# Mask products and shared banks for the score maxima, a re-measured planner, and another order of the query blocks

## The reference, cut to what matters

```
scores = q @ k^T                      # per head, 2048 x 2048
scores = where(j <= i, scores, -inf)  # causal
scores += slope[h] * (j - i)          # attention a only
w = softmax(scores / 4);  out = (w @ v) @ Wo + bo
x = x + out
```

## Time and profile before

| | us |
|---|---|
| median of 3 runs (2376.23 to 2398.64) | 2376.96 |
| the profiled execution | 2381.28 |
| its span, first to last instruction | 2379.6 |
| attention cores up to the last turn | 87 to 543 and 1282 to 1731 |
| from there to the experts' first work | 543 to 591 and 1731 to 1779 |
| the experts and the projections | the rest |
| mean granted clock of PE | 0.912 |

### The profile page before, as it was taken

How to read it: one execution, slowest core, us unless ns; L and a number is a source line. 1 busy time by engine, 2 the same in 40 slices (tenths; PEclk the granted TensorE clock), 3 DMA queues, 4 the chain that set the end, 5 groups by cost and what they waited for, 6 DMA issues and landing times. The chain is left out here.

```text
span 2379.6 us, 33652 instructions
## 1 busy us (share of the span) xinstructions
PE 2189.3 (92%) x11000; PEld 1442.5 (61%) x11000; DVE 1619.7 (68%) x3265; ACT 962.1 (40%) x1333; POOL 727.2 (31%) x722
## 2 busy tenths in 40 slices
PE   5699999997799998999987999999977999999998
PEld 4444444444588887888764444444445888878886
DVE  6578887874665556666566788878746666666665
ACT  1145756475222232322341467564742322322222
POOL 4000101002355554555340001010023555545553
PEclk9678988898899999999996689888988999999999
DMA  3640404000133332333126404040002333333332
GB/s 136 130 58 2 55 2 55 2 2 18 65 122 108 108 104 91 108 110 115 66 97 125 55 2 54 2 54 2 2 8 77 120 108 108 104 122 110 108 108 77
DMA packets 59956, 172.46 MB, mean 72 GB/s; under 512 B 7912, under 2 KB 13560, under 8 KB 57360
## 3 DMA queue, kind: packets, MB, share of 16 engines
q1 hardware_dynamic: 59852, 171.14, 27.5%
HBM read 150.35 MB, written 20.23 MB: 72 GB/s over the span
## 5 line engine op out<-in xcount | busy, mean ns | idle before, releaser
L850 ACT ACTIVATE probs_t<-exp_banks 128x1024 f32<-128x1024 f32 (+3 forms) x640 | 539.3, 895 | 346.0 <-PE exp_banks L1099 340.6
L976 PE MATMUL exp_banks<-xT_t,e_hi_t 128*128 128x512 f32 x2080 | 656.0, 396 | 15.2 <-DVE inter_t L1227 13.4
L1363 DVE TENSOR_REDUCE chunk_max_t<-max_bank 128x1 f32<-128x512 f32 x768 | 488.5, 683 | 95.8 <-PE max_bank L1078 93.1
L976 PEld LDWEIGHTS exp_banks<-xT_t,e_hi_t 128*128 128x128 f32 x2080 | 393.2, 190 | 107.8 <-issue 13.1
L659 POOL TENSOR_TENSOR e_hi_t<-e_raw_t,ones_t 128x512 fp32r<-128x512 f32 (+1 forms) x260 | 283.9, 1092 | 534.3 <-PE pv_bank L976 455.2
L976 PE MATMUL exp_banks<-xT_t,e_lo_t 128*128 128x512 f32 x1040 | 412.0, 396 | 0.0
L1236 DVE TENSOR_TENSOR i_lo_t<-inter_t,i_hi_t 128x512 fp32r<-128x512 f32 (+1 forms) x264 | 249.6, 945 | 184.4 <-ACT i_hi_t L787 184.4
L787 ACT ACTIVATE i_hi_t<-inter_t 128x512 fp32r<-128x512 f32 (+1 forms) x264 | 166.9, 632 | 508.4 <-DVE inter_t L1231 508.4
L753 POOL TENSOR_SCALAR_AFFINE_SELECT probs_t<-probs_t 128x512 f32<-128x512 f32 x128 | 81.4, 638 | 909.3 <-ACT probs_t L850 909.3
L1113 PE MATMUL pv_bank<-probs_t,values_t 128*32 128x512 f32 (+3 forms) x2560 | 327.1, 587 | 14.2 <-POOL probs_t L753 10.1
L1227 DVE TENSOR_TENSOR inter_t<-exp_banks,silu_t 128x512 f32<-128x512 f32 (+1 forms) x264 | 182.3, 690 | 201.5 <-ACT silu_t L783 198.8
(11 more groups left out here) (200 smaller groups left out, 2061.7 us busy)
## 6 DMA issues: line engine op xcount, KB each, us to landing
wide_t<-route_rows SPq DMA_DIRECT2D x128, 512.0 KB, 4.4
e_raw_t<-in_experts SPq DMA_DIRECT2D x130, 384.0 KB, 4.3
Qp_t<-q_parts SPq DMA_DIRECT2D x36, 256.0 KB
Kp_t<-k_parts SPq DMA_DIRECT2D x24, 256.0 KB
q_parts<-part_hi_t SPq DMA_DIRECT2D x16, 256.0 KB, 2.6
q_parts<-part_lo_t SPq DMA_DIRECT2D x16, 256.0 KB, 3.1
k_parts<-part_hi_t SPq DMA_DIRECT2D x16, 256.0 KB, 3.0
k_parts<-part_lo_t SPq DMA_DIRECT2D x16, 256.0 KB, 3.4
```

Source lines behind the costliest of these rows:

```text
L850: act.activation(probs[:, e % NP, 2 * p:2 * p + 2, off:QB], exp_banks[p][:, :, off:QB], ACT.Exp, scale=D ** -0.5).then_inc(exp_done, 1)
L976: last = pe.matmul(out, stationary(a, k), moving(c, k), start=start and n == 0, stop=stop and n == len(order) - 1, skip_group_check=not (s ...
L1363: dve.tensor_reduce(to, bank[:, 0:n], AX.X, ALU.max).then_inc(max_free, 1)
```

## The change

1. **Mask products.** The custom instruction goes. The mask is now added by PE: after the product of a diagonal piece, two more products (a half of an identity, bf16, by a half of the triangle `cut`, 128 and 64 columns wide) accumulate -1e30 onto the last 128 keys. DVE uses the plain reduction throughout. POOL makes the bf16 copies at the start, eight more small copies, and PE waits for them before the first core.
2. **Shared banks.** The 16 diagonal pieces of a block share 10 banks: the two 256-wide pieces of a head half in one bank (one reduction for both), a 384-wide and a 128-wide piece in one bank (two reductions), each 512-wide one alone.
3. **The plan's model** has other durations, models the two halves of PE and POOL's cut, and lets `turned` come 2600 ns after the turn. `LOAD` stays 12000 ns.
4. **The order of blocks** becomes 0123, 3210, 3210, 3201 for groups 0 to 3. The load of group g + 1 still follows the turn of the third block in order.

```diff
-UP, DOWN = list(range(NB)), list(range(NB))[::-1]
-BLOCKS = [(g, b) for g in range(G) for b in (UP if g < G - 1 else DOWN)]
+UP, DOWN, LAST = [0, 1, 2, 3], [3, 2, 1, 0], [3, 2, 0, 1]
+ORDER = [UP, DOWN, DOWN, LAST]
+BLOCKS = [(g, b) for g in range(G) for b in ORDER[g]]
...
+def bank_items(b):
+
+    full = [(hh, [(p, r, c)]) for r in range(TPB) for c in range(b) for p in range(2) for hh in range(2)]
+    diagonal = [(hh, [(0, 1, b), (1, 1, b)]) for hh in range(2)]
+    diagonal += [(hh, [(p, 2, b), (p, 0, b)]) for p in range(2) for hh in range(2)]
+    diagonal += [(hh, [(p, 3, b)]) for p in range(2) for hh in range(2)]
+    return full + diagonal
...
-    SIGNAL, ROWS_BACK, LOAD = 250, 7000, 12000
+    SIGNAL, ROWS_BACK, LOAD, CYCLE = 45, 2600, 12000, 2.3
+    WEIGHTS, TURN, CTX, PROJECT = 183, 300, 550, 1600
...
+        items = [("max", g, b, k) for k in range(len(bank_items(b)))]
+        if number:
+            items.insert(2, ("turn", *BLOCKS[number - 1]))
...
+            _, g, b, number = item
+            hh, parts = bank_items(b)[number]
+            issue = halves(start, [(hh, part_width(b, r, c)) for _, r, c in parts])
+            for _, _, c in parts:
+                ended[hh] += 60 * (c == b)
+            pe = max(ended)
+            dve = max(dve, ended[hh] + SIGNAL)
+            if parts[0][1:] == (1, b):
+                dve += 152 + QB / 0.96
+            else:
+                for _, r, c in parts:
+                    dve += 152 + part_width(b, r, c) / 0.96
...
             turned[item[1:]] = dve + ROWS_BACK
+            if item[2] == ORDER[g][NB - 2] and 1 <= g < G - 1:
+                loaded[g + 1] = max(turned[item[1:]], scored_group.get(g - 1, dve)) + LOAD
...
         elif kind == "qk":
-            act = max(act, pe + SIGNAL, free) + 2 * n / 1.2 + 60
+            act = max(act, pe + SIGNAL, free) + 170 + 2 * n * 0.832
...
-                    if b == NB - 2 and 1 <= g < G - 1:
+                    if b == ORDER[g][NB - 2] and 1 <= g < G - 1:
...
+                            if c == b:
+                                rows = slice(hh * HALF, (hh + 1) * HALF)
+                                for a in range(2):
+                                    last = pe.matmul(bank[:, end - P + a * HALF:end], ident16[rows, a, :],
+                                                     cut16[rows, a, a * HALF:P], start=False, stop=a == 1)
...
-                            dve.tensor_tensor_reduce(masked[k % 2][:, 0:n], bank[:, 0:n], diag_mask[:, QB - n:QB],
-                                                     1.0, VLOW, ALU.add, ALU.max, to).then_inc(max_free, 1)
+                                op = dve.tensor_reduce(chunk_max[:, slot, 2 * p + hh, r, c:c + 1], bank[:, begin:end],
+                                                       AX.X, ALU.max)
```

More of the change, by code:

```diff
@@ L73, with part_width @@
 LOADS_AFTER = {"K0": "fresh", "Q1": 0, "K1": 1}
+def bank_items(b):
[4 more added lines that the diff above has]
+    return full + diagonal
+def part_width(b, r, c):
+    return P * (r + 1) if c == b else QB
 def core_plan():
-    SIGNAL, ROWS_BACK, LOAD = 250, 7000, 12000
+    SIGNAL, ROWS_BACK, LOAD, CYCLE = 45, 2600, 12000, 2.3
+    WEIGHTS, TURN, CTX, PROJECT = 183, 300, 550, 1600
     maxima = []
     for number, (g, b) in enumerate(BLOCKS):
[L92 to L98, removed]
+        items = [("max", g, b, k) for k in range(len(bank_items(b)))]
+        if number:
+            items.insert(2, ("turn", *BLOCKS[number - 1]))
+        maxima += items
     maxima.append(("turn", *BLOCKS[-1]))
@@ L141, in ready, with halves, whole @@
             return None
-        return exps.get((item[4], 1))
+        if (item[4], 1) not in exps:
+            return None
+        return max(exps[item[4], 1], pv_bank_free) if item[3] == 0 else exps[item[4], 1]
+    def halves(start, widths):
+        at_issue = start
+        for hh, n in widths:
+            weights = max(at_issue, began[hh])
+            began[hh] = max(weights + WEIGHTS, ended[hh] + 8)
+            ended[hh] = began[hh] + n / CYCLE
+            at_issue = weights + 3
+        return at_issue
+    def whole(end):
+        began[:], ended[:] = [end, end], [end, end]
+        return end
     while any(at[k] < len(s) for k, s in enumerate(streams)):
@@ L149, in core_plan @@
                 if when is not None:
-                    when = max(when, pe)
+                    same = mode == "halves" and s[at[k]][0] in ("max", "qk")
+                    when = max(when, issue if same else max(issue, pe))
                     if best is None or when < best[0]:
@@ L195, in core_plan @@
             n = width(b, j)
-            pe = start + n / 2.4 + 20
+            issue = halves(start, [(0, n), (1, n)])
+            pe = max(ended)
             free = products[e - NP] if e >= NP else 0
-            act = max(act, pe + SIGNAL, free) + 2 * n / 1.2 + 60
[L199 to L202, removed]
+            act = max(act, pe + SIGNAL, free) + 170 + 2 * n * 0.832
+            exp_bank_free[scored % 2] = act + 50
+            scored += 1
+            exps[e, p] = act + 50
+            if p == 1 and j >= TPB * b:
+                pool = max(pool, act + 50) + 740
+                exps[e, p] = pool + 50
+            if p == 1 and b == ORDER[g][-1] and j == TPB * (b + 1) - 1:
+                scored_group[g] = pe
         elif kind == "pv":
@@ L397, in build @@
         total_units = u
[L399 removed]
+        order_of = {phase: LAST if i and phases[i - 1][0] != "f" else UP for i, phase in enumerate(phases)}
         bias_of_col = {"q": 0, "k": 2, "v": 4, "upk": 6, "kl": 8, "vl": 9}
@@ L417, in build, with sq_exp @@
                     n += 1
+        sq_of = {}
+        for item in plan:
+            if item[0] == "qk":
+                sq_of[item] = len(sq_of)
+        SQ = len(sq_of)
+        def sq_exp(layer, g, b, j, p):
+            return layer * SQ + sq_of["qk", g, b, j, p, e_of[0, g, b, j]]
         mu_of = {}
```

167 lines of the change are left out of this document (93 added, 74 removed).

## The result

The changed kernel takes **2471.15 us** (2467.79 to 2481.44, four runs): 1.0351 times the kernel before, 95% interval 1.0269 to 1.0434. It is slower by 3.5%; the forecast was 2441 and slower by 2.7%. The ratio goes by the kernel before as measured beside it, where a fourth run had lifted its median to 2387.8; against 2376.96, from which the forecast was made, it would be 4.0%. The profiled execution took 2470.07 us, with a span of 2468.4 and a granted clock of 0.897 on average.

The account below looks back on a forecast made before the run. DVE's maxima were taken to set the pace, PE close behind. Terms 88 - 5 + 46 - 10 - 20 - 10 - 20 - 5 = +64 on 2381.3 gave 2445, forecast 2441 us; 8-in-10 range 2350 to 2505.

Parts of the forecast that it names:

- load exposed: At changes of group: DVE has no maximum for 22 us, twice in each core, until the load arrives; +88 us.
- units in the wait: Before PE stops at the late load, it makes some 4 units with no maximum beside them; -5 us.
- mask products: Diagonal pieces: two extra weight loads and products on PE, costing 0.136 us for 338 pieces; +46 us (14 to 91).
- DVE's own work: Diagonal pieces on DVE: a block's reductions fall from 7.75 to 7.43 us, 32 x 0.32; -10 us.
- shared banks: Diagonal pieces: 16 hand-overs per block become 10, so DVE's 53.8 us idle before them shrinks in proportion; -20 us (0 to -54).
- the plan: Old and new model both give three maxima per unit, so the 96 us idle before full chunks mostly stays; -10 us.
- order's other side: Descending block order in the cores: fewer pure stretches, five ways back into mixed work fewer; -20 us (0 to -45).
- tail: Behind the last turn: 12 units left either way; a 4.6 us wait of `pv` for POOL may go or return; -5 us.
- masks lie open: Rival, diagonal pieces: weight loads and products uncovered, 0.45 us for each of 338, 152 us instead of 46; 2547 us, chance 0.11.
- Three banks are the real limit: Rival, faster: two thirds of DVE's 150 us idle before maxima go (-100); 2339 us, chance 0.17.
- The parts cancel: Rival, whole kernel: masks at 14, 50 us of idle gone, 15 from the order; +17, 2394 us, chance 0.14.
- The new plan does not do what its name says: Rival, plan's model: LOAD is 12 where the rows have 27, ratio of three kept; inside the forecast, no separate chance.

## Why the prediction was right or wrong

**The ledger.** Each part is a difference of two kernels, in ratio times 2377:

| part | predicted | measured | difference of |
|---|---|---|---|
| load exposed, units in the wait | +83 | +108 | new order with the load after the first block, and changed kernel |
| mask products, DVE's own work | +36 | +38 | kernel before, and masks alone |
| shared banks | -20 | -30 | masks alone, and masks and banks with the old plan |
| the plan | -10 | -34 | masks and banks with the old plan, and the old order in the changed kernel |
| order's other side | -20 | +1 | old order in the changed kernel, and new order with the load after the first block |
| tail | -5 | not separated (+5 by the traces, below) | |
| sum | +64 | +83 | |

The direction and the cause were right. That the sum fits to 20 us is in part luck: load and order were 46 us too low, banks and plan 34 us too high. The single parts also depend on the order in which they are taken, as the mask products show below.

**The load** was the right step, and its size too small: 26.6 us a time where I had 22. PE could start 33.1 us after the turn (291.99 to 325.09), where I had 30. I had read the end of the load from the DMA share of one stretch, as if it stopped at once at 404.6. It thins out instead, in both kernels (before, then after; same columns as the stages):

```profile
405.00:406.00 1.00, 1.00 (x14) 0.61 (x7) 0.77 (x4) 0.46 (x1) 0.00 (x0) 1.00 0.22 49
406.00:407.00 1.00, 1.00 (x13) 0.25 (x9) 1.00 (x4) 0.83 (x1) 0.00 (x0) 1.00 0.04 8
```
```profile
322.00:323.00 1.00, 0.00 (x0) 0.00 (x0) 0.00 (x0) 0.00 (x0) 0.00 (x0) 0.50 0.15 25
323.00:324.00 1.00, 0.00 (x0) 0.00 (x0) 0.00 (x0) 0.00 (x0) 0.00 (x0) 0.50 0.13 41
```

So the load before lasted to 407, some 32 us from its turn, and the reader comes a little behind that. Block 0's maxima took 6.8 us of the 8 that I gave them, and DVE's first maximum starts 0.9 us behind PE's product. The -5 for units run in the wait was not there: DVE's idle time in the cores is 115 us above that of the kernel with the load after the first block (275.5 and 160.4), 9 more than the four gaps.

PE's stop of 15.4 us came as 17.67. I had called it part of the cost ("all scores and sums behind it stop too"), but charged only DVE's gap, and rightly so: with the plan told of 27.4 us the stop is 15 us shorter and the time the same.

**Mask products.** In a mixed round at full clock of the changed kernel:

```profile
287.49 1.06 PE L1187 MATMUL pv_bank<-probs_t,values_t 128*32 128x512 f32 x8
...
289.48 0.27 PE L1145 MATMUL max_bank<-Kp_t,Qp_t 50*128 50x256 f32 x1
289.60 0.26 PE L1151 MATMUL max_bank<-cut_t,ident_t 64*128 64x128 bf16 x2
289.69 0.36 PE L1145 MATMUL max_bank<-Kp_t,Qp_t 50*128 50x256 f32 x1
289.90 0.26 PE L1151 MATMUL max_bank<-cut_t,ident_t 64*128 64x128 bf16 x2
290.08 1.07 PE L1187 MATMUL pv_bank<-probs_t,values_t 128*32 128x512 f32 x8
```

The round is 2.59 us where the earlier trace rows have 2.08. It has as many score columns for maxima (three times 512) and five diagonal pieces, so the products cost about 0.10 us a piece, where I took 0.136. The four lines in the middle are one shared bank, so all their products are of one head and lie in one half of the array. From the first score product to the second, with two mask products between them, there are 0.21 us, and from the first to the next `pv` 0.60. The weight loads of these six products take 0.19 us for scores and 0.098 for a mask. The five behind the first alone are 0.58 of the 0.60 us, so if they stood by themselves next to nothing would be left for the products. Loads therefore lie beside products of their own half, at least in part. The rival "masks lie open" is out: it wanted 152 us, and the dearest measurement is 50 (idle time with masks alone). The Trainium skill's rule that a load overlaps running matmuls only if its row group differs (TensorE: Matmul & The Clock Gate, "The mechanism") does not hold in this stretch; the same section also lets a load go ahead when it targets a background weight buffer, and the stretch agrees with that. The Trainium skill's other rule, that non-fp32 weights load about twice as fast ("Weight-path perf modes"), agrees with the trace: 98 ns for 184. Weight loads of the mask and of the scores, min/median/max ns:

```profile
L1151 PEld LDWEIGHTS max_bank<-cut_t,ident_t x1024: 92/98/148, 77.9 to 1814.4; 64*128 64x128 bf16 x171
```
```profile
L1145 PEld LDWEIGHTS max_bank<-Kp_t,Qp_t x640: 182/184/334, 190.2 to 1814.1; 50*128 50x128 f32 x80, 48*128 48x128 f32 x80
```

But the term depends on the plan, which I had not seen. Under the old plan the products add 50.5 us of idle time. Under the new one, which books 60 ns for each piece, they add 12 (old order, against DVE's own masking) to 17.5 (changed kernel), and my +46 is too much there. The table books the difference under "the plan".

**DVE's own work.** Predicted -10, and busy time in the cores fell by 15.0 us.

**The plan.** "Either way three maxima per unit", hence -10: this step failed. The ratio of three was not what the new model changes. In the kernel before it *cost* 17 us; with mask products and shared banks it gave 34. Since the banks gave 30 and 33 us under either plan, the difference lies with the mask products: they cost 38 us under the old plan and nothing that can be told under the new one. Which entry of the model does it was not tried; the 60 ns that it books for a piece are the likely one. Its DVE price of 685 ns was also wrong, and mending it went with 21 us less, 7 of them in the profiled cores. I wrote that "PE makes no more per round" and left the 96 us before full chunks alone. Half clock in the cores (312.6 us before, 289 with the old order, 260 after mending the price) speaks for more mixed rounds having been to be had.

**Shared banks.** -30 and -33 where I had -20. I scaled by the number of hand-overs of the pieces alone. With DVE's own masking the traces give 42 us of idle time less (187.4 to 145.7), and 54 was the upper end that I had named. Part of it may come from the pieces' new place in the block.

**The order's other side.** -20 predicted, nothing measured. "Fewer falls of the clock" was right for the order only once the load is hidden (257 us at half clock for 289), and then it paid nothing that can be told. In the changed kernel itself half clock rose to 399.5 us: each gap starves PE too. My price, two waits of 2 us for each way back into mixed work, came from one stretch and was not a mean.

**The eight copies on POOL** were costed at nothing, by POOL's idle time. They gave 8 us, by a way that I had not looked at (below).

**The tail** is inside its bounds: 49.9 and 49.8 us from the last turn to the last addition, 47.4 before in both cores. That is +5 where I had -5.

**The rivals.** "Three banks are the real limit" wanted over 85 of the 150 us of idle time gone. Outside of the four gaps 141.7 us stand before maxima, where I expected 120. The rival is out for the changed kernel. There is something in it behind the masks: with them in place banks and plan together gave 64 us, of which the masks had cost 38 before. "The parts cancel" is what the kernel does with the load after the first block (0.9896). "The new plan does not do what its name says" was true of LOAD (14.6 us from the turn, for 33.1) and harmless there.

**Signs that I had named.** Gaps of about 20 us with a full DMA share, PE waiting for the load for some 15 us: there, 26.6 and 17.7. Rest of the idle time near 120 us: 141.7, above it. Diagonal rounds longer by 0.2 to 0.4: the one shown, with five pieces, is longer by 0.5. Fewer falls of the clock: not in the changed kernel.

**Open.** Why the new model costs 17 us in the kernel before wasn't tried item by item. A kernel with the mended price, the new order and the load after the first block wasn't run either.

## What to carry to other kernels

When the order of work changes, list every prefetch that hangs on "the block before the last", and compare what is left behind it with the transfer's time to its reader, not to the point at which its traffic thins out. In a plan made of durations, check the spacing at which an engine takes work as well as the duration of one instruction (here 0.60 and 0.68 us), and look for instructions that have no entry: a model mended in one place can lose time until the kernel does what it assumes. A stop of an engine that is off the bound need not be a cost; the idle time of the engine that sets the pace is. Here DVE's busy time in the cores hardly moves from kernel to kernel (729 to 754 us), while its idle time goes from 146 to 276 us, so nearly all that the cores gain or lose is idle time.

## What the runs showed of the hardware, unexpected

**An addition on POOL stretched one on DVE.** In the prologue of the kernel before:

```profile
35.15 9.03 POOL L744 TENSOR_TENSOR x_sb_t<-x_sb_t,bias_rows_t 128x4096 f32<-128x4096 f32 x1
36.78 7.67 DVE L1319 TENSOR_TENSOR slope_lo_t<-slope_raw_t,slope_hi_t 128x256 fp32r<-128x256 f32 x1
```

and of the changed kernel:

```profile
36.22 0.41 DVE L1393 TENSOR_TENSOR slope_lo_t<-slope_raw_t,slope_hi_t 128x256 fp32r<-128x256 f32 x1
37.74 9.05 POOL L806 TENSOR_TENSOR x_sb_t<-x_sb_t,bias_rows_t 128x4096 f32<-128x4096 f32 x1
```

The same subtraction takes 7.67 us when it starts inside POOL's addition, and ends with it (44.45 and 44.18); it takes 0.41 when it starts first. The eight small copies push POOL's addition behind it, and the first maximum comes at 79.0 instead of 87.4. All kernels with the copies have these 8 us (first maximum at 78.4 to 80.2), and those without start at 85.9 or later. The Trainium skill has the rule (SBUF — State Buffer, "Who interferes with whom"): a DVE instruction with two SBUF inputs and a GpSimd instruction that reads SBUF exclude each other for a whole instruction, and the one that starts first goes first. Both traces agree with it.

**A load with nothing beside it is no faster.** The stretch 295 to 327 of the changed kernel, in which DVE works 4.43 us and PE 13.77, and 377 to 409 of the kernel before, with 21.84 and 31.17, each hold one whole load. Its rate, the last number of each line, is the same:

```profile
295.00:327.00 32.00, 13.77 (x111) 5.32 (x109) 4.43 (x9) 12.11 (x16) 2.54 (x4) 0.74 0.83 101
```
```profile
377.00:409.00 32.00, 31.17 (x154) 13.15 (x157) 21.84 (x51) 17.20 (x19) 0.63 (x1) 0.68 0.84 102
```
